# One transformer layer on one core: batches of three score groups, nine copied groups a unit, and a new order on VectorE

## The chip, the cores and the metric

The kernel runs on one core of a Trainium2 chip. A core has TensorE (matmuls; called PE in the profile, with its weight loads as PEld), ScalarE (ACT, here nearly only the exponentials), VectorE (DVE), GpSimd (POOL) and the queues that start DMAs (SyncE is SP). The engines run side by side, each through its own list of instructions in order, and wait for each other on semaphores. The metric is the device time of one launch in microseconds (us); lower is better.

## The reference

The input is x, 4096 tokens of 256 numbers, float32. `xn` is its layer norm. The output is x + attention(xn) + FFN(xn):

```
q, k, v = xn @ Wq.T, xn @ Wk.T, xn @ Wv.T          # 16 heads of 16 numbers
attention = softmax(q @ k.T / 16) @ v               # per head, 4096 x 4096 scores
scores = softmax(xn @ gate_w.T); idx = top2(scores + gate_b)
expert(x) = silu((x@w1 + b1) * (x@w3 + b3)) @ w2 + b2   # 256 -> 352 -> 256
FFN = sum over the two chosen of 8 experts of score * expert(xn)  +  shared expert(xn)
```

The work is dominated by the attention: 16 heads x 4096 x 4096 exponentials, with a small product before (q by k, 16 deep) and after each (by v, 16 wide).

## The kernel before, in words

**Attention.** A head is worked through in two sweeps, one for each half of the queries. A sweep has 32 key tiles of 128 keys (`NT`), and each key tile two score groups. A score group is 128 keys by 1024 queries: TensorE makes it with two matmuls side by side in the two halves of its rows (line 894) into two PSUM banks. There are three such pairs of banks (`SB = 3`), so group n goes where group n - 3 was. ScalarE then writes exp(group) to one of 8 slots of `probs` in SBUF (line 1198). A value step (line 907) is one key tile: it multiplies two finished groups by v, in four column strips, and adds into the one output bank (`O_BANK`). A program has 2048 score groups and 1024 value steps. The trace counts 8 matmuls per value step and 2 per score group.

**Copied groups.** For some groups (`moved(n)`) VectorE first copies the scores from PSUM to the `probs` slot (line 1773), which frees the PSUM pair; ScalarE then takes the exponential from SBUF in place (line 1194). TensorE's next use of that pair waits for the copy (`s_moved`) and not for the exponential (`s_exp`).

**FFN units.** The FFN is cut into 55 units of up to 256 tokens: 8 of the shared expert, 39 of routed tokens (the last seven, units 40 to 46, get narrower in steps of 32 columns), 8 of the shared expert. One unit is woven into 36 score groups and 18 value steps. It has three upward parts (`up_both(u, 0..2)`, line 919, 12 matmuls each) and the downward part of the unit before (`down_tile`, line 931, 18 matmuls). All go through one bank (`F_BANK`), which VectorE reads: `gate` and `product` after each upward part, `keep` after the downward part. VectorE also splits all weights and tokens into a high and a low part (`up_hi`, `up_lo`, `down_hi`, `down_lo`, `tokens_hi`, `tokens_lo`), and ScalarE adds one tanh a unit.

**Order.** It is written out by hand. On TensorE `unit(u)` is a list of `next_scores(count)`, `next_values(count)` and FFN parts. I call a run of score groups with what follows it up to the next run a batch. On VectorE a loop over u lists the FFN steps, `move_scores(u, place)` for each copied place of the unit, and `after_values(m)`, which does what is due once m value steps are finished: `take_output` (line 1620, a transpose that empties the output bank at the end of a sweep), `add_output` two value steps later, and `next_v` (v of the next head). Before the first value step of a sweep TensorE waits for `take_output` (`s_osb`). The two wait rules that matter are these:

```
# next_scores: group n needs the pair of group n - 3
if n >= SB and moved(n - SB): pe.wait_ge(s_moved, moved_up_to(n - SB))
elif n >= SB:                 pe.wait_ge(s_exp, n - SB + 1)
# next_values: value step m needs groups 2m and 2m + 1
if issued[2] < 2 * m + 2:     pe.wait_ge(s_exp, 2 * m + 2)
```

**Tail.** From unit 49 on no group is copied before (`MOVE_TO = 49`). There VectorE also joins the experts' rows into the result (`join`, five tiles a unit, each two operations), with rows that GpSimd gathers.

Below, places are counted from 0 within a unit's 36 groups, in the order in which `unit(u)` issues them. The copied places before are 11, 14, 20, 23, 31 and 34 (the code's numbers are one higher, and `moved` takes the one off).

## Time and profile before

| what | value |
|---|---|
| median of 3 runs | 2106.71 us (2106.71 to 2111.02) |
| profiled execution: time, span of the core | 2107.03 us, 2105.1 us |
| TensorE matmuls busy | 2076.8 us, 99% |
| ScalarE busy | 2008.4 us, 95% |
| VectorE busy | 1141.8 us, 54% |
| granted TensorE clock, mean | 0.999 of full |
| copy of a score group (L1773), mean | 1222 ns |
| transpose of the output bank (L1620) | 0.71 us |
| `add_output`, three operations | 0.25, 0.42 and 0.43 us, 1.15 us from start to end |
| `down_hi` and `down_lo` | 0.55 and 0.96 us |
| one tile of `join`, two operations | 0.48 us each, 1.03 us together |

Matmuls are pipelined and their ends are modelled, so 99% says that TensorE hardly ever had nothing in flight, not that it ran at its peak. The difference of two start times is the safer number: it is the pace. The same holds for ScalarE, where an exponential lasts 1.05 us but the next starts earlier. All times below are from the one profiled execution.

### The profile page before, as it was taken

The page shows a single profiled execution, that of the slowest core. Times are in us where ns is not written, and L with a number is a line of the kernel's source. Part 1 is how long each engine was busy: PE and PEld are TensorE (multiplying, and loading weights), DVE is VectorE, ACT ScalarE, POOL GpSimd, SP SyncE. Part 2 cuts the span into 40 slices and gives each one's busy share as a digit, 9 for nine tenths or more (in the row PEclk, how much of TensorE's full clock was granted, in tenths as well). Part 3 has the DMA queues.
Part 4 walks back from the last instruction along what each step waited for, and adds up shares of the span by engine and source line. Part 5 has one row for each costly group of instructions (what it writes and reads, how often), then busy time and mean ns, then how long its engine had stood idle before and what let it go on. Part 6 is the DMA issues. An engine that isn't in the chain of part 4 may idle for free.

```text
span 2105.1 us, 38572 instructions
## 1 busy us (share of the span) xinstructions
PE 2076.8 (99%) x15722; PEld 968.1 (46%) x15722; DVE 1141.8 (54%) x1843; ACT 2008.4 (95%) x2228; POOL 250.7 (12%) x260
## 2 busy tenths in 40 slices
PE   9999999999999999999999999999999999999998
PEld 6734444444444444444444444444444444444442
DVE  8554555555555555555555555555555554544531
ACT  6799999999999999999999999999999999999998
POOL 0307764000000000000000000000000000122220
PEclk9999999999999999999999999999999999999999
DMA  8874433222222212132222231313132221323331
GB/s 290 284 257 120 123 123 102 60 57 70 67 73 63 71 49 81 52 79 61 65 60 72 67 73 55 85 44 80 52 80 62 70 70 57 100 73 89 99 99 35
DMA packets 223352, 187.82 MB, mean 89 GB/s; under 512 B 110471, under 2 KB 192190, under 8 KB 223174
## 3 DMA queue, kind: packets, MB, share of 16 engines
q1 hardware_dynamic: 209350, 148.68, 25.0%
q0 software_dynamic: 12496, 36.34, 5.3%
q8 instruction: 124, 2.03, 0.4%
q14 instruction: 54, 0.44, 0.1%
q10 hardware_dynamic: 1328, 0.33, 0.1%
HBM read 130.21 MB, written 55.05 MB: 88 GB/s over the span
## 4 chain that ended last, share of the span: by engine, by line
PE 88%; ACT 6%; DVE 4%; DMA 1%; issue 1%; SPq 0%; another core or an unknown queue 0%; DVEq 0%; ACTq 0%
PE PS L907 41%; PE PS L894 28%; PE PS L919 12%; PE PS L931 6%; ACT probs L1198 5%; ACT probs L1194 1%; DMA qk_parts<-part_a 1%; DVE probs L1773 1%; DVE stats L1324 0%; DVE o_t L1620 0%; PE PS L684 0%; DVE probs L1348 0%; DVE x_parts L1360 0%; PE PS L798 0%; DVE w_hi L1688 0%
## 5 line engine op out<-in xcount | busy, mean ns | idle before, releaser
L1198 ACT ACTIVATE probs<-PS 128x1024 f32<-128x1024 f32 x1766 | 1679.6, 1053 | 58.0 <-PE PS L894 45.6
L907 PE MATMUL PS<-probs,v_head 128*32 128x512 f32 x8192 | 989.6, 599 | 10.7 <-DVE o_t L1620 7.2
L894 PE MATMUL PS<-q_ring,k_stack 50*128 50x512 f32 x4096 | 697.8, 436 | 6.4 <-ACT probs L1198 4.6
L894 PEld LDWEIGHTS PS<-q_ring,k_stack 50*128 50x128 f32 x4096 | 333.5, 184 | 542.1 <-ACT probs L1198 471.6
L1773 DVE COPY probs<-PS 128x1024 f32<-128x1024 f32 x282 | 344.6, 1222 | 186.7 <-PE PS L894 185.7
L907 PEld LDWEIGHTS PS<-probs,v_head 128*32 128x32 f32 x8192 | 210.0, 108 | 482.1 <-issue 372.8
L1194 ACT ACTIVATE probs<-probs 128x1024 f32<-128x1024 f32 x282 | 301.4, 1069 | 2.4 <-DVE probs L1773 2.1
L1661 DVE TENSOR_SCALAR gate_in<-PS,bias_sb 128x256 f32<-128x256 f32 (+7 forms) x165 | 76.3, 463 | 370.9 <-PE PS L919 364.0
L919 PE MATMUL PS<-x_hi,w_hi 128*128 128x256 f32 (+9 forms) x660 | 199.3, 302 | 0.0
L1270 POOL DMA_DIRECT2D slot_y<-y_sb x39 | 27.9, 716 | 1387.3 <-DVE y_sb L1731 1351.7
L919 PE MATMUL PS<-x_hi,w_lo 128*128 128x256 f32 (+9 forms) x660 | 184.4, 279 | 0.0
L919 PE MATMUL PS<-x_lo,w_hi 128*128 128x256 f32 (+9 forms) x660 | 184.2, 279 | 0.0
L919 PEld LDWEIGHTS PS<-x_hi,w_hi 128*128 128x128 f32 (+1 forms) x660 | 118.6, 180 | 58.1 <-issue 58.1
L1671 DVE SCALAR_TENSOR_TENSOR hid<-hid,prod 128x768 f32<-128x768 f32 (+7 forms) x55 | 49.9, 907 | 131.4 <-ACT hid L1179 131.4
L919 PEld LDWEIGHTS PS<-x_lo,w_hi 128*128 128x128 f32 (+1 forms) x660 | 118.8, 180 | 0.0
L919 PEld LDWEIGHTS PS<-x_hi,w_lo 128*128 128x128 f32 (+1 forms) x660 | 118.8, 180 | 0.0
L931 PE MATMUL PS<-w_hi,hid_hi 128*128 128x256 f32 (+4 forms) x318 | 95.4, 300 | 0.0
L1692 DVE TENSOR_TENSOR w_lo<-w_raw,w_hi 128x1408 fp32r<-128x1408 f32 x55 | 89.9, 1635 | 0.2
L931 PE MATMUL PS<-w_lo,hid_hi 128*128 128x256 f32 (+4 forms) x318 | 89.8, 282 | 0.0
L931 PE MATMUL PS<-w_hi,hid_lo 128*128 128x256 f32 (+4 forms) x318 | 89.7, 282 | 0.0
L1666 DVE SCALAR_TENSOR_TENSOR prod<-PS,bias_sb,gate_in 128x256 f32<-128x256 f32 (+7 forms) x165 | 76.8, 466 | 5.9
L1261 POOL DMA_INDIRECT slot_x<-y_sb,pos x64 | 73.9, 1155 | 19.1 <-issue 14.0
(201 smaller groups left out, 1238.8 us busy)
## 6 DMA issues: line engine op xcount, KB each, us to landing
w_raw<-in_w SPq DMA_DIRECT2D x110, 352.0 KB
k_stack<-qk_parts SPq DMA_DIRECT2D x120, 128.0 KB
w_raw<-in_w SPq DMA_DIRECT2D x55, 256.0 KB
q_ring<-qk_parts SPq DMA_DIRECT2D x372, 32.0 KB
qk_parts<-part_a SPq DMA_DIRECT2D x20, 512.0 KB, 4.9
slot_x<-early_sq SPq DMA_DIRECT2D x39, 256.0 KB, 3.6
slot_in<-slot_x SPq DMA_DIRECT2D x156, 64.0 KB, 2.5
slot_y<-y_sb POOLq DMA_DIRECT2D x39, 256.0 KB, 2.5
```

What stands on the lines that cost most here:

```text
L894: last = pe.matmul(bank(2 * score_buffer(turn, g) + r), k_stack[rows, kt * P:(kt + 1) * P], q_ring[rows, sweep, i * QC:(i + 1) * QC], star ...
L907: last = pe.matmul(bank(O_BANK)[VW * j:VW * (j + 1), :], v_head[:, kt, :], probs[:, slot, (j % 2) * QC:(j % 2 + 1) * QC], start=(kt == 0), ...
L919: last = pe.matmul(f_half(w)[0:FT[j], 0:width(u)], a[u % 2][:, w, dt, j * P:j * P + FT[j]], b[:, dt * CH:dt * CH + width(u)], start=(n == ...
L931: last = pe.matmul(f_half(t)[0:own, :], a[0:rows, j, t * P:t * P + own], b[0:rows, j, :], start=(n == 0), stop=(n == 8))
L1194: nc.scalar.activation(probs[:, prob_slot(g), :], probs[:, prob_slot(g), :], ACT.Exp, scale=ENERGY_SCALE).then_inc(s_exp, 1)
L1198: nc.scalar.activation(probs[:, prob_slot(g), :], bank(2 * score_buffer(h, g), 2), ACT.Exp, scale=ENERGY_SCALE).then_inc(s_exp, 1)
L1261: nc.gpsimd.indirect_dma_start(out=slot_x, out_offset=bass.IndirectOffsetOnAxis(ap=pos[:, u * TPU + t, k:k + 1], axis=0), in_=rows[:, t, : ...
L1661: V.tensor_scalar(gate_in[0:FT[j], 0:width(u)], f_half(0)[0:FT[j], 0:width(u)], bias_sb[0:FT[j], u % 2, j:j + 1], 0.5, ALU.add, ALU.mult). ...
L1666: V.scalar_tensor_tensor(prod[u % 2][0:FT[j], j, 0:width(u)], f_half(1)[0:FT[j], 0:width(u)], bias_sb[0:FT[j], u % 2, 3 + j:4 + j], gate_i ...
L1671: V.scalar_tensor_tensor(hid[:, :, 0:width(u)], hid[:, :, 0:width(u)], 1.0, prod[u % 2][:, :, 0:width(u)], ALU.add, ALU.mult).then_inc(s_h ...
L1692: V.tensor_tensor(w13_lo[u % 2][:, :, :, :], w13_raw[:, :, :, :], w13_hi[u % 2][:, :, :, :].bitcast(f32), ALU.subtract).then_inc(s_w13, 1)
L1773: V.tensor_copy(probs[:, prob_slot(g), :], bank(2 * score_buffer(h, g), 2)).then_inc(s_moved, 1)
```

## The change: three groups in every batch, other copied places, another order on VectorE

On TensorE a unit becomes twelve batches of three groups. Before it had thirteen (ten of three, three of two). The eighteen value steps follow in eight runs, two of three and six of two; before it was nine of two. The first unit starts one group earlier, and the one group left over stands behind the last unit.

```
-FIRST_GROUPS = 2 * FIRST_VALUES + 3
+FIRST_GROUPS = 2 * FIRST_VALUES + 2
-TANH_AT = 39
-MOVED = (12, 15, 21, 24, 32, 35)
+TANH_AT = 41
+MOVED = (2, 8, 17, 20, 23, 26, 29, 32, 35)
-MOVE_TO = 49
+MOVE_TO = 55
 def unit(u):
-    next_scores(2)
+    next_scores(3)
     up_both(u, 0)
-    next_scores(2)
-    next_values(2)
+    next_scores(3)
+    next_values(3)
     next_scores(3)
     up_both(u, 1)
-    next_scores(2)
-    next_values(2)
     next_scores(3)
-    next_values(2)
-    next_scores(3)
-    next_values(2)
+    next_values(3)
     next_scores(3)
...
-    next_scores(2)
+    next_scores(3)
     up_both(u, 2)
...
-    next_scores(1)
+    next_scores(3)
+    next_values(2)
```

The copied places are now 2, 8, 17, 20, 23, 26, 29, 32 and 35: the last group of nine of the twelve batches. Copies run from unit 2 to unit 54. On VectorE `take_output` leaves `after_values` and becomes `take_values(m)`, and the loop is listed anew:

```
+def take_values(m):
+    if (m - 1) % NT + 1 == NT:
+        take_output((m - 1) // NT)
 for u in range(UNITS + 1):
+    move_scores(u, 2)
     gate(u, 0); product(u, 0)
+    take_values(m + 2); after_values(m + 2); join(u, 1); move_scores(u, 8)
+    gate(u, 1); product(u, 1); hidden(u - 1); take_values(m + 4)
+    hidden_hi(u - 1); hidden_lo(u - 1); take_values(m + 6); after_values(m + 4)
+    up_hi(u + 1); up_lo(u + 1); keep(u - 1); move_scores(u, 17); after_values(m + 6)
+    down_hi(u); down_lo(u); take_values(m + 8); move_scores(u, 20); after_values(m + 8); join(u, 1)
+    take_values(m + 10); move_scores(u, 23); turn_tokens(u + 1); after_values(m + 10)
+    take_values(m + 12); move_scores(u, 26); gate(u, 2); product(u, 2); move_scores(u, 29)
+    after_values(m + 12); tokens_hi(u + 1); take_values(m + 14); tokens_lo(u + 1)
+    move_scores(u, 32); after_values(m + 14); join(u, 1); take_values(m + 16)
+    move_scores(u, 35); after_values(m + 16); join(u, 2); take_values(m + 18); after_values(m + 18)
```

TensorE's list from the end of a unit's first upward part to its second, before:

```order
L919 MATMUL PS<-x_hi,w_lo 128x256
L894 MATMUL PS<-q_ring,k_stack 128x512 x4
L907 MATMUL PS<-probs,v_head 32x512 x8
L894 MATMUL PS<-q_ring,k_stack 128x512 x6
L919 MATMUL PS<-x_hi,w_hi 128x256
```

The same place now:

```order
L919 MATMUL PS<-x_hi,w_lo 128x256
L894 MATMUL PS<-q_ring,k_stack 128x512 x6
L907 MATMUL PS<-probs,v_head 32x512 x12
L894 MATMUL PS<-q_ring,k_stack 128x512 x6
L919 MATMUL PS<-x_hi,w_hi 128x256
```

Two score matmuls are one group and four value matmuls one value step in this list. The run of two groups has become one of three, and the run of two value steps one of three.

VectorE's list in unit 34, from the copy behind the third upward part on; a sweep ends before the unit's seventeenth value step. Before:

```order
L1773 COPY probs<-PS 128x1024 [waits s_scores]
L1712 CAST x_hi<-x_t 128x512 [waits s_ab,s_tt]
L1716 TENSOR_TENSOR x_lo<-x_t,x_hi 128x512 [waits s_xhi]
L1773 COPY probs<-PS 128x1024 [waits s_scores]
L1620 STREAM_TRANSPOSE o_t<-PS 128x512 [waits s_pv]
L1500 COPY v_head<-v_all 128x8x16 [waits s_pv]
L1625 RECIPROCAL rec<-o_t 128x16 [waits s_osb]
```

Now:

```order
L1774 COPY probs<-PS 128x1024 [waits s_scores]
L1710 CAST x_hi<-x_t 128x512 [waits s_ab,s_tt]
L1714 TENSOR_TENSOR x_lo<-x_t,x_hi 128x512 [waits s_xhi]
L1774 COPY probs<-PS 128x1024 [waits s_scores]
L1618 STREAM_TRANSPOSE o_t<-PS 128x512 [waits s_pv]
L1774 COPY probs<-PS 128x1024 [waits s_scores]
L1498 COPY v_head<-v_all 128x8x16 [waits s_pv]
L1623 RECIPROCAL rec<-o_t 128x16 [waits s_osb]
```

The transpose now stands ahead of the copy of the last batch (place 35) and behind that of the batch before it. Before, it stood behind the copy of the last batch.

VectorE's list in unit 24, where a sweep ends before the unit's fifth value step. Before:

```order
L1666 SCALAR_TENSOR_TENSOR prod<-PS,bias_sb,gate_in 128x256 [waits s_gin]
L1620 STREAM_TRANSPOSE o_t<-PS 128x512 [waits s_pv]
L1688 CAST w_hi<-w_raw 128x1408 [waits s_w13r]
L1773 COPY probs<-PS 128x1024 [waits s_scores]
L1500 COPY v_head<-v_all 128x8x16 [waits s_pv]
L1625 RECIPROCAL rec<-o_t 128x16 [waits s_osb]
L1627 TENSOR_TENSOR early_sq<-o_t,rec 128x256 [waits s_loop_a]
L1632 TENSOR_TENSOR resid<-resid,early_sq 128x16x16 [waits s_resid,s_norm]
L1773 COPY probs<-PS 128x1024 [waits s_scores]
```

Now, from the hidden step to the first copy behind the downward weights:

```order
L1669 SCALAR_TENSOR_TENSOR hid<-hid,prod 128x768 [waits s_tanh]
L1618 STREAM_TRANSPOSE o_t<-PS 128x512 [waits s_pv]
L1674 CAST hid_hi<-hid 128x512 [waits s_hid]
...
L1774 COPY probs<-PS 128x1024 [waits s_scores]
L1498 COPY v_head<-v_all 128x8x16 [waits s_pv]
L1623 RECIPROCAL rec<-o_t 128x16 [waits s_osb]
L1625 TENSOR_TENSOR early_sq<-o_t,rec 128x256 [waits s_loop_a]
L1630 TENSOR_TENSOR resid<-resid,early_sq 128x16x16 [waits s_resid,s_norm]
L1694 CAST w_hi<-w_raw 128x768 [waits s_w2r]
L1698 TENSOR_TENSOR w_lo<-w_raw,w_hi 128x768 [waits s_w2h]
L1774 COPY probs<-PS 128x1024 [waits s_scores] x2
```

The fifth value step now lies inside a run of three (steps 4 to 6), so nothing of TensorE's stands between the end of the sweep and the step that waits for the transpose. And `add_output` now stands, with the split of the downward weights, between the copies of places 17 and 20.

## Rows read from the trace of the kernel before

**Rows 1.** Chain of work that ended last, unit 25: start us, us, engine and line, matmuls.
```profile
1003.35 1.62 PE PS L919 x12
1004.98 0.66 PE PS L894 x4
1005.64 1.85 PE PS L907 x16
1007.49 0.89 PE PS L894 x6
...
1010.00 0.78 PE PS L894 x4
...
1019.02 2.35 PE PS L931 x18
...
1030.28 1.59 PE PS L919 x12
...
1038.26 1.62 PE PS L919 x12
```

**Rows 2.** Timeline of ScalarE, unit 25: start, us, engine, line, count, [idle before <-releaser].
```profile
1007.48 0.92 ACT L1179 ACTIVATE hid<-prod 128x768 f32<-128x768 f32 x1
1008.21 6.83 ACT L1198 ACTIVATE probs<-PS 128x1024 f32<-128x1024 f32 x7
...
1021.84 1.94 ACT L1198 ACTIVATE probs<-PS 128x1024 f32<-128x1024 f32 x2 [0.34 <-PE PS L894]
```

**Rows 3.** Timeline of TensorE and VectorE, same unit, behind the downward part.
```profile
1021.30 0.96 PE L894 MATMUL PS<-q_ring,k_stack 50*128 50x512 f32 x6
...
1022.31 1.22 DVE L1773 COPY probs<-PS 128x1024 f32<-128x1024 f32 x1 [0.21 <-PE PS L894]
```

**Rows 4.** Timeline of ScalarE near the end, an unbroken run of exponentials.
```profile
2073.93 24.86 ACT L1198 ACTIVATE probs<-PS 128x1024 f32<-128x1024 f32 x27 [1.62 <-PE PS L894]
```

**Rows 5.** Timeline of unit 25, a score group that waits for an exponential.
```profile
1010.27 0.19 PEld L894 LDWEIGHTS PS<-q_ring,k_stack 50*128 50x128 f32 x2 [0.16 <-ACT probs L1198]
```

**Rows 6.** Timeline of unit 8, a value step that waits for an exponential.
```profile
417.89 0.96 PE L894 MATMUL PS<-q_ring,k_stack 50*128 50x512 f32 x6
417.92 1.06 ACT L1194 ACTIVATE probs<-probs 128x1024 f32<-128x1024 f32 x1 [0.32 <-DVE probs L1773]
...
418.89 1.92 ACT L1198 ACTIVATE probs<-PS 128x1024 f32<-128x1024 f32 x2
...
419.94 0.16 PEld L907 LDWEIGHTS PS<-probs,v_head 128*32 128x32 f32 x8 [1.01 <-ACT probs L1198]
...
420.70 1.06 ACT L1194 ACTIVATE probs<-probs 128x1024 f32<-128x1024 f32 x1
...
420.94 0.96 PE L894 MATMUL PS<-q_ring,k_stack 50*128 50x512 f32 x6
421.65 2.85 ACT L1198 ACTIVATE probs<-PS 128x1024 f32<-128x1024 f32 x3
```

**Rows 7.** Timeline of unit 34, the end of a sweep.
```profile
1350.19 1.22 DVE L1773 COPY probs<-PS 128x1024 f32<-128x1024 f32 x1 [0.46 <-PE PS L894]
1351.33 0.71 DVE L1620 STREAM_TRANSPOSE o_t<-PS 128x512 f32<-128x512 f32 x1
...
1352.09 1.92 PE L907 MATMUL PS<-probs,v_head 128*32 128x512 f32 x16 [1.94 <-DVE o_t L1620]
```

**Rows 8.** Chain of work, unit 49, where no group is copied.
```profile
1852.70 1.12 PE PS L894 x6
```

**Rows 9.** Timeline of TensorE: first upward part of units 2, 40, 49 and 54.
```profile
192.84 0.39 PE L919 MATMUL PS<-x_hi,w_hi 128*128 128x256 f32 x1
...
1530.01 0.37 PE L919 MATMUL PS<-x_hi,w_hi 128*128 128x224 f32 x1
...
1840.60 0.39 PE L919 MATMUL PS<-x_hi,w_hi 128*128 128x256 f32 x1
...
2021.96 0.39 PE L919 MATMUL PS<-x_hi,w_hi 128*128 128x256 f32 x1
```

More of the change, by code:

```diff
@@ L110, in moved @@
 def moved(n):
-    u, place = divmod(n - FIRST_GROUPS + 1, UNIT_GROUPS)
+    u, place = divmod(n - FIRST_GROUPS, UNIT_GROUPS)
     return MOVE_FROM <= u < MOVE_TO and place in MOVED
@@ L121, in moved_group @@
 def moved_group(u, place):
-    return unit_start(u) - 1 + place
+    return unit_start(u) + place
 def shared_loads(u):
@@ L1045, in _ @@
                 unit(u)
+            next_scores(1)
             for n in range(6):
@@ L1754, in after_values @@
                     add_output(n - 1)
-                if kt == NT:
-                    take_output(n)
-                elif n % 2 == 1 and n < SWEEPS - 1 and kt % KTB == 0:
+                if kt < NT and n % 2 == 1 and n < SWEEPS - 1 and kt % KTB == 0:
                     next_v(n // 2, kt // KTB - 1)
+            def take_values(m):
+                if (m - 1) % NT + 1 == NT:
+                    take_output((m - 1) // NT)
             def join(u, count):
@@ L1789, in _ @@
                     product(u, 0)
+                take_values(m + 2)
+                after_values(m + 2)
+                join(u, 1)
+                move_scores(u, 8)
+                if real:
+                    gate(u, 1)
+                    product(u, 1)
                 if u:
                     hidden(u - 1)
-                after_values(m + 2)
+                take_values(m + 4)
                 if u:
@@ L1795, in _ @@
                     hidden_lo(u - 1)
-                if real:
-                    gate(u, 1)
-                    product(u, 1)
+                take_values(m + 6)
                 after_values(m + 4)
@@ L1801, in _ @@
                     up_hi(u + 1)
-                move_scores(u, 12)
-                after_values(m + 6)
-                move_scores(u, 15)
-                if more:
                     up_lo(u + 1)
-                after_values(m + 8)
-                join(u, 2)
                 if u == 0:
@@ L1822, in _ @@
                     counts()
-                after_values(m + 12)
+                take_values(m + 8)
+                move_scores(u, 20)
+                after_values(m + 8)
                 join(u, 1)
+                take_values(m + 10)
+                move_scores(u, 23)
                 if routed(u + 1):
                     turn_tokens(u + 1)
-                after_values(m + 14)
+                after_values(m + 10)
+                take_values(m + 12)
+                move_scores(u, 26)
                 if real:
@@ L1830, in _ @@
                     product(u, 2)
-                move_scores(u, 32)
+                move_scores(u, 29)
+                after_values(m + 12)
                 if more:
                     tokens_hi(u + 1)
+                take_values(m + 14)
+                if more:
                     tokens_lo(u + 1)
@@ L1838, in _ @@
                     experts_of_tiles()
+                move_scores(u, 32)
+                after_values(m + 14)
+                join(u, 1)
+                take_values(m + 16)
                 move_scores(u, 35)
                 after_values(m + 16)
-                join(u, JOINS - 3)
+                join(u, 2)
+                take_values(m + 18)
                 after_values(m + 18)
```

8 lines of the change are left out of this document (4 added, 4 removed).

## The prediction

> **What bounds the kernel now.** I read the page first (TensorE 99% busy, ScalarE 95%, VectorE 54%), then the chain of waits over one ordinary unit, then the timelines of ScalarE and VectorE beside it, and last the starts of all units. In the chain of unit 25 every piece is TensorE's [rows 1]. The reader should see the pace: a batch of three groups takes 0.89, of two 0.66, a run of two value steps 1.85, an upward part 1.62 (the third 1.59), the downward part 2.35. Ten of three, three of two, nine value runs, the FFN parts: 8.9 + 2.0 + 16.7 + 4.8 + 2.35 = 34.75, and one group that waits 0.12 (0.78 instead of 0.66). The unit lasts 1038.26 - 1003.35 = 34.91. So an ordinary unit is bound by TensorE. ScalarE is close behind. Exponentials from PSUM come every (24.86 - 1.04) / 26 = 0.916 [rows 4], a tanh takes 1008.21 - 7.48 = 0.73 [rows 2]. A copied group costs more: from 417.92 to 418.89 is 0.97, though the next scores were there at 418.43, and from 420.70 to 421.65 it is 0.95 with the next there at 421.48 [rows 6]; I take 0.95. That makes 30 x 0.916 + 6 x 0.95 + 0.73 = 33.9 of the 34.9. The missing 1.0 are idle gaps behind the three FFN parts, of which the row behind the downward part shows one [rows 2].
>
> This is a loop of two engines that each have under 3% to spare. The copies and the waits decide which one yields.
>
> **Four delays that I need.** Let T be the start of a batch. (a) The first group reaches ScalarE at T + 0.54 (1021.30 to 1021.84), the third reaches VectorE at T + 1.01, its copy lasts 1.22 and ScalarE starts some 0.13 later, so T + 2.36 [rows 2, 3]. (b) A score group starts 1.15 after the start of the exponential that frees its banks: the sixth group's began at 1008.21 + 0.91 = 1009.12, the load follows at 1010.27 [rows 2, 5]. Groups two and three of a batch start at T + 0.23 and T + 0.46 when nothing holds them. (c) A value step starts 1.05 after its exponential (418.89 to 419.94) and then needs 1.00 to the end of the run [rows 6]. The batch of that row began at 417.89 and should have handed over at 417.89 + 0.89 + 1.85 = 420.63; it did at 420.94. So the second value step of a pair holds TensorE once its exponential starts later than T + 0.69. (d) From the end of a sweep's last value step to the first of the next, the transpose between them included, is 0.9: 0.76 from the transpose's start (1351.33 to 1352.09) [rows 7], and some 0.13 before it as in (a).
>
> **Part 1: fewer switches on TensorE.** A group costs 0.89 - 0.66 = 0.23, so a batch carries 0.20 besides its groups. A value step costs 1.85 - 1.00 = 0.86, so a run carries 0.13. One batch and one run less: -0.33. A run of three is not in the trace; it lies between 1.85 + 0.86 = 2.71 and two runs' price of 1.85 + 1.00 = 2.85. I take 2.71, the nearer rows. The unit becomes 12 x 0.89 + 6 x 1.85 + 2 x 2.71 + 4.8 + 2.35 = 34.4 if nothing waits, 0.45 less than 34.91 with the 0.12 of today gone too. With the upper price it is 34.7.
>
> **Part 2: what ScalarE takes back.** Three exponentials with a copied one need 2 x 0.916 + 0.95 = 2.78, uncopied 2.75. Follow a unit, with b how late ScalarE is against T + 0.54. Behind the downward part (batch length 0.89 + 2.35 = 3.24) it is on time. Three batches with a pair of value steps last 2.75 each, and b grows to 0.05 to 0.09. The batch with the third upward part lasts only 0.89 + 1.59 = 2.48 and now brings three groups instead of two: b = 0.35. After two more batches b is 0.40, and there the last pair needs the exponential of place 33, started at T + 0.54 + 0.40 = T + 0.94. By (c) TensorE waits 0.25. The next two upward parts (2.51 a batch) push b up again, while a run of three (3.6) lets ScalarE catch up. On the way (b) caps b near 0.40: a second group waits 0.03 to 0.04 in the batch of place 4 and about 0.12 in that of place 10. The run of three itself does not wait: its third step is due at T + 0.89 + 1.72, its exponential starts by T + 0.94. Sum of waits 0.40 of the 0.45 gained. An ordinary unit becomes 34.83 (34.45 + 0.38), 0.07 less than before. From the other side: 27 x 0.916 + 9 x 0.95 + 0.73 = 34.0 of work and 0.5 idle in each of the two long batches at places 9 and 12 is 34.9 to 35.0. I keep 34.83, with 34.45 and 34.98 as ends. Over units 2 to 39: -0.07 x 38 = -2.7, ends -17 and +3.
>
> On the copies the Trainium skill has a rule against this change (VectorE: DVE Perf Modes, section on the TRN2 errata): ScalarE pays 224 cycles besides the elements when it reads SBUF and 172 when it reads PSUM, at 1.2 GHz. The trace agrees: 0.95 to 0.97 against 0.916. By that rule three more copied groups cost 3 x 0.043 = 0.13 a unit, by the rows 3 x 0.034 to 0.054, and my sum would be 1 us longer over these units.
>
> **Part 3: VectorE's order.** Copies add 3 x 1.22 = 3.7 to some 20 a unit, which VectorE has. What counts is whether each starts at T + 1.01. In an ordinary unit I find it does: the dense stretch (second gate, hidden parts, upward weights, `keep`) now holds no copy, and the split of the downward weights ends 1.5 behind the copy of place 17, about 0.1 before that of place 20 is due. So this costs nothing, with 0.1 to spare there.
>
> At the end of a sweep it does count. Before, the first upward parts of units 2 and 40 are 1337.17 apart [rows 9]; 38 x 34.90 = 1326.2, so 11.0 is lost. Three times 2.0 of it are units 2, 18 and 34, where the transpose stood behind a copy: in unit 34 the copy starts at 1350.19, the transpose at 1351.33, and TensorE stood idle for 1.94 [rows 7]. Those 6.1 go: the transpose is now ahead. So do 0.7 to 1.6 in each of units 4 and 20 and 36. Against that:
> - Units 17 and 33: the sweep ends inside a run of three, with no batch between. By (d) 0.9 plus the 0.13 of a new run, 1.0 each.
> - Units 8, 24 and 40: the same, and `add_output` (1.15) plus the downward weights (1.5) now stand between the copies of places 17 and 20. The copy is 1.1 late and ScalarE with it, so the pair with place 21 waits about 0.8 more: 2.0 each.
> - Units 6, 22 and 38: the transpose waits behind `down_lo` and comes at T + 0.9 instead of T + 0.13: 0.85 each.
> - Units 11, 13, 27, 29: 0.1 to 0.3 each.
>
> Units 2 to 39: 2.0 + 4.0 + 2.55 + 0.8 = 9.4 against 11.0, that is -1.6. Ends: -6, if late copies find slack, and +5, if each of these turns costs a whole 2.0.
>
> **Part 4: the rest.** Units 40 to 48 took 310.6 [rows 9]. The narrow ones are near ScalarE's limit (about 34.1 a unit), so little changes, and unit 40 gets a late sweep: +1.0. Units 49 to 53 took 181.4, 36.3 each [rows 9]. Without copies three or four batches a unit wait 0.23 (1.12 instead of 0.89) [rows 8]; these waits go. With `join` squeezed in the copy of place 2 is 0.5 late, about +0.35 a unit. At 34.83 + 0.35 and 1.0 for the sweep in unit 49, five units take 177, -4.3. But some 2.6 of the 181.4 are two hold-ups of TensorE's batches in units 49 and 51 that no copy explains, and I can't say that they go; I take -3.0, ends 0 and -5. Start, units 0 and 1, and tail: +0.5.
>
> **Sum.** -2.7 - 1.6 + 1.0 - 3.0 + 0.5 = -5.8 against this execution's 2107.03 (span 2105.1), which is 0.3 above the median: 2101.2 us.
>
> **The rivals.** First, TensorE stays the bound and ScalarE keeps up. For it: ScalarE has 1.0 idle a unit today, and the loss of 0.25 hangs on a threshold read at one place. Against it: three groups behind the third upward part are one more than before. It gives 34.45 a unit: -17 instead of -2.7, 2087. Second, on the other side: the sweep ends. VectorE's late copies and a transpose with nothing to cover it cost 2.0 in each of the eight units 6, 8, 17, 22, 24, 33, 38 and 40, 16 against the 11.0 lost before, the ordinary unit stays at 34.9 and the late units give nothing: with 0.8 for the small turns and 0.5 at the ends about +6, 2113. For it: before, a transpose behind one copy cost 2.0 [rows 7]. Against it: the same order frees the units that lost most. It decides, at 34.9 a unit, once these eight cost over 1.2 each on average. Third, nothing measurable: ScalarE takes back all of part 1 (34.9) and the late units gain as little as the sweeps lose, 2106.
>
> **How the numbers follow.** A measurement of this kernel can tell about 0.2%, 4.2 us: faster is below 2102.5. My forecast has 0.5, with a spread of 4 about it: 0.3 faster, 0.19 the same, 0.01 slower. The first rival has 0.2 (faster), the second 0.17 (0.03 the same, 0.14 slower), the third 0.13 (0.11 the same, 0.02 slower). Together 0.5 faster, 0.33 the same, 0.17 slower. The range of 2089 to 2111 leaves out the better half of the first rival and the worse half of the second.
>
> **What would show it.** Right, if the chain of an ordinary unit shows the last pair of value steps (place 33) longer than 1.85 and ScalarE idle only behind the two runs of three and the downward part; if the unit lasts 34.8; if the 2.9 batches of units 2, 18 and 34 are gone; and if units 8 and 24 show a late copy of place 20. Wrong, if ScalarE still idles behind the third upward part (then 34.5), if a run of three takes over 2.8, or if a copy in an ordinary unit starts after T + 1.1.

## The result, and the profile after

The changed kernel takes 2117.88 us (median of 5 runs, 2116.30 to 2120.46). The kernel before, run beside it, takes 2109.18 (2106.71 to 2113.64). The ratio is 1.0041, 95% interval 1.0025 to 1.0058: slower by 0.4%, where 2101.2 and a gain were forecast. The profiled execution took 2117.15 (span 2115.2) against 2107.03 of before, +10.1.

The busy times of the page do not show where that is: TensorE and ScalarE are as busy as before. The chain of work that ended last does look different. From the page of the changed kernel, parts 1 and 4, and part 4 of the kernel before:

```profile
PE 2070.7 (98%) x15722; PEld 974.3 (46%) x15722; DVE 1378.8 (65%) x2038; ACT 2006.8 (95%) x2228; POOL 244.9 (12%) x260
...
PE 50%; ACT 42%; DVE 5%; issue 1%; another core or an unknown queue 1%; DMA 1%; SPq 0%; DVEq 0%; ACTq 0%
...
PE 88%; ACT 6%; DVE 4%; DMA 1%; issue 1%; SPq 0%; another core or an unknown queue 0%; DVEq 0%; ACTq 0%
```

ScalarE's share has gone from 6% to 42%, and 1% is time whose end nothing in the trace explains ("another core or an unknown queue"). The starts of the units show where the time went. These rows of TensorE's timeline, changed kernel, are the first upward parts of units 2, 40, 49 and 54 and answer [rows 9]:

```profile
194.37 0.38 PE L919 MATMUL PS<-x_hi,w_hi 128*128 128x256 f32 x1
...
1525.73 0.37 PE L919 MATMUL PS<-x_hi,w_hi 128*128 128x224 f32 x1
...
1838.34 0.39 PE L919 MATMUL PS<-x_hi,w_hi 128*128 128x256 f32 x1
...
2028.73 0.39 PE L919 MATMUL PS<-x_hi,w_hi 128*128 128x256 f32 x1
```

From such differences, in every profiled execution (us; the last column runs to the end of the span):

| kernel | set | units 0, 1 | 2 to 39 | 40 to 48 | 49 to 53 | unit 54 and tail |
|---|---|---|---|---|---|---|
| before | 0 | 70.9 | 1337.2 | 310.6 | 181.4 | 83.1 |
| changed | 1 | 73.4 | 1331.4 | 312.6 | **190.4** | **86.5** |
| spread_joins | 2 | 73.4 | 1330.7 | 312.5 | 176.5 | 83.1 |
| late_nocopy | 2 | 73.4 | 1331.3 | 313.9 | 183.1 | 83.4 |
| before_burst | 2 | 70.9 | 1338.0 | 310.6 | 190.9 | 83.0 |
| direct_rows | 2 | 73.4 | 1331.3 | 312.6 | 176.9 | 82.7 |
| paced_gathers | 3 | 73.4 | 1331.0 | 312.5 | 176.9 | 82.8 |
| sweep_order | 3 | 73.4 | 1327.7 | 313.2 | 190.6 | 85.9 |
| short_tanh | 3 | 73.4 | 1328.9 | 313.7 | 194.2 | 86.0 |
| spread_turns_from_1 | 3 | 72.0 | 1328.2 | 311.8 | 183.4 | 83.4 |
| burst_alone | 4 | 73.4 | 1331.3 | 312.6 | 176.9 | 82.8 |
| burst_no_copies | 4 | 73.4 | 1330.7 | 314.2 | 183.0 | 83.4 |
| paced_order_from_1 | 4 | 71.8 | 1328.2 | 311.8 | 177.3 | 82.1 |
| thin_joins | 5 | 73.4 | 1330.7 | 312.5 | 175.1 | 82.7 |
| few_rows | 5 | 73.4 | 1330.7 | 312.5 | 176.9 | 82.7 |

"Set" says which kernels were run together, from set 1 on with the kernel before beside them; set 0 are the three runs of the kernel before ahead of the prediction (median 2106.71 us), from which its trace is. Beside the others the kernel before took 2109.18 us in set 1, 2104.40 in set 2, 2109.31 in set 3, 2103.97 in set 4 and 2102.73 in set 5. The changed kernel itself was run in set 1 alone. This matters for the late units, as shown below.

So the body gained 5.8 and the late units lost 9.0, the tail 3.3, the first two units 2.5, units 40 to 48 2.0. The start gained 1.0.

**The ordinary unit** lasts what was forecast. The chain of the changed kernel in unit 25, beside [rows 1] (start us, us, engine and line, count):

```profile
1004.18 2.71 PE PS L907 x24
...
1009.40 0.97 PE PS L894 x6
1010.37 2.71 PE PS L907 x24
...
1013.98 2.35 PE PS L931 x18
1016.33 0.45 PE PS L894 x2
...
1016.80 1.94 ACT probs L1196 x2
1018.74 0.95 ACT probs L1192
1019.68 1.82 ACT probs L1196 x2
...
1033.56 0.92 ACT probs L1196
1034.48 0.04 issue
1034.52 1.06 PE PS L907 x8
```

A run of three value steps takes 2.71. The batch of place 9 takes 0.97 instead of 0.89. The last pair starts at 1033.38 and the next scores at 1035.52, 2.14 instead of 1.85; the chain shows its second step waiting for the exponential. And from the first group behind the downward part (1016.80) to that exponential's end (1034.48) the chain is ScalarE's alone: 17.7 of the unit's 34.8 us. TensorE sets the pace in the other half, with the runs of three and the first, second and downward FFN parts. So the unit now has two halves with different limits, where before all of it was TensorE's [rows 1]. In ScalarE's half three exponentials with a copied one take 2.77 (1.82 and 0.95), while TensorE needs 2.75 for a batch with a pair of value steps and 2.48 for the one with the third upward part. ScalarE falls behind by that, until the last pair waits 0.29 for it. A saving on TensorE in that half would buy nothing. ScalarE's timeline there has only two gaps, one behind a run of three and one behind the downward part, beside [rows 2]:

```profile
1010.28 2.99 ACT L1196 ACTIVATE probs<-PS 128x1024 f32<-128x1024 f32 x3
1013.55 2.86 ACT L1196 ACTIVATE probs<-PS 128x1024 f32<-128x1024 f32 x3 [0.27 <-PE PS L894]
1016.80 1.94 ACT L1196 ACTIVATE probs<-PS 128x1024 f32<-128x1024 f32 x2 [0.39 <-PE PS L894]
```

Unit 34, which stood 1.94 [rows 7], now takes the transpose ahead of the copy; TensorE's next value steps follow 0.77 later, and the unit lasts 34.81:

```profile
1347.09 0.72 DVE L1618 STREAM_TRANSPOSE o_t<-PS 128x512 f32<-128x512 f32 x1 [0.65 <-PE PS L907]
1347.86 2.21 PE L907 MATMUL PS<-probs,v_head 128*32 128x512 f32 x16
1347.95 1.22 DVE L1774 COPY probs<-PS 128x1024 f32<-128x1024 f32 x1
```

**The late units.** Units 49 to 53 take 35.89, 38.49, 36.65, 39.30 and 40.06 (before 36.72, 35.87, 37.10, 35.96, 35.71). I call it a hold-up when TensorE's results reach the other engines late and TensorE then runs dry. Timeline behind the start of unit 52 (1949.37), changed kernel:

```profile
1952.60 0.48 DVE L1743 SCALAR_TENSOR_TENSOR resid<-y_sb,weight,resid 128x256 f32<-128x256 f32 x1
...
1954.60 0.96 PE L894 MATMUL PS<-q_ring,k_stack 50*128 50x512 f32 x6
1954.67 0.87 ACT L1177 ACTIVATE hid<-prod 128x768 f32<-128x768 f32 x1
...
1958.27 1.94 ACT L1196 ACTIVATE probs<-PS 128x1024 f32<-128x1024 f32 x2 [2.73 <-remote]
1958.42 1.23 DVE L1774 COPY probs<-PS 128x1024 f32<-128x1024 f32 x1 [5.34 <-remote]
1959.35 0.50 PE L894 MATMUL PS<-q_ring,k_stack 50*128 50x512 f32 x2 [2.17 <-ACT probs L1196]
...
1961.20 4.12 PE L907 MATMUL PS<-probs,v_head 128*32 128x512 f32 x24
```

The three score groups were issued at 1954.60. By the four delays of the prediction ScalarE should have had the first at 1955.14 (it was done with its tanh at 1955.54) and VectorE the third at 1955.61. Both got theirs at 1958.3 and 1958.4, together; "remote" means that the trace has no releaser for that moment. The trace does keep the moments at which TensorE's signals for finished score groups came: 1958.25, 1958.29 and 1958.33, and the signal for the upward part issued behind them at 1958.46. In unit 25 such signals are 0.23 apart, and an upward part takes TensorE 1.62. Three groups 0.04 apart and an upward part 0.13 behind them can't be the pace of the work. It was done by then, and the signals came late and all at once. TensorE then ran dry. The granted clock also fell, after TensorE had been idle from 1957.2 to 1959.3. The columns are window, its length, busy time (count) of PE, PEld, DVE, ACT and POOL, clock, DMA share, GB/s.

```profile
1954.00:1958.00 4.00, 3.17 (x26) 1.97 (x18) 0.00 (x0) 1.54 (x2) 2.21 (x3) 1.00 0.59 174
1958.00:1962.00 4.00, 2.24 (x10) 0.68 (x14) 3.51 (x6) 3.73 (x5) 0.00 (x0) 0.82 0.12 45
1962.00:1966.00 4.00, 4.00 (x30) 1.21 (x22) 3.76 (x6) 2.10 (x4) 0.00 (x0) 0.76 0.00 0
```

1.00 is the 2.4 GHz level; 0.82 and 0.76 are stretches partly at 1.2 GHz, and the run of three at 1961.20 took 4.05 to the next scores, not 2.71. Such hold-ups end at 1883.2 (named "PE PS L894" by the trace), 1921.3, 1958.3, 1993.3 to 1995.3 and 2037. Beside each of them GpSimd was issuing indirect gathers for `join` without a break, in the same stretch:

```profile
1946.25 0.95 POOL L1298 DMA_INDIRECT y_sb<-slot_y,pos  x1 [8.66 <-DVE resid L1743]
...
1949.53 1.01 POOL L1298 DMA_INDIRECT y_sb<-slot_y,pos  x1 [0.30 <-PE PS L894]
1950.85 0.95 POOL L1298 DMA_INDIRECT y_sb<-slot_y,pos  x1 [0.30 <-issue]
...
1955.87 0.95 POOL L1298 DMA_INDIRECT y_sb<-slot_y,pos  x1 [0.30 <-issue]
```

That is a run of six 1.25 apart, with two more and a plain load just ahead. From unit 49 on the kernel before had eleven runs of four and none longer. The change made the longer runs: of five tiles a unit it joins one behind copy 32, two behind copy 35 and one behind the next unit's value steps (1945.0 to 1953.1 in this stretch), and each join frees a buffer for two gathers.

**Where the late signals appear.** Late signals are in the traces of sets 0, 1 and 3 alone. The rows below are read from the recorded moments of TensorE's score signals. "Latest" is the longest time, from unit 48 on, between the start of a group's last matmul and its signal; the signal behind the last scores of the kernel is left out. In units 10 to 39 it is 0.52 at most in every trace. The last column counts the recorded signals of units 1 to 4, 144 groups whose place lies long before any join.

| set | time of before | kernel | longest run of gathers | smallest distance of two signals | latest | recorded in units 1 to 4 |
|---|---|---|---|---|---|---|
| 0 | 2106.71 | before | 4 | 0.04 | 1.97 | 132 |
| 1 | 2109.18 | changed | 8 | 0.04 | 4.31 | 127 |
| 3 | 2109.31 | sweep_order, short_tanh | 8 | 0.04 | 4.55, 4.44 | 123, 126 |
| 3 | | spread_turns_from_1 | 4 | 0.04 | 1.58 | 125 |
| 3 | | paced_gathers | 2 | 0.04 | 0.57 | 129 |
| 2, 4, 5 | 2102.73 to 2104.40 | all nine | up to 10 | 0.22 | 0.65 | 144 each |

In sets 2, 4 and 5 no signal was late, in no kernel and with runs of up to ten gathers, and the kernel before took 2.3 to 6.6 us less. What differs between the sets is not known; sets 3 and 4 ran on the same chip. So kernels of sets 0, 1 and 3 can be compared, and there the signals are the later the longer the run of gathers is. But a hold-up that is missing in a kernel of sets 2, 4 or 5 may be missing because of the set: the changed kernel was not run beside it.

### The profile page after: what moved, and what is told of

The parts are those of the page before. It is cut to its first block, busy times and chain, and to the rows that moved or that the text cites. A ratio compares the mean times of both kernels' runs of the same rounds, so it can differ in the third digit from the quotient of the medians.

```text
span 2115.2 us, 38791 instructions
## 1 busy us (share of the span) xinstructions
PE 2070.7 (98%) x15722; PEld 974.3 (46%) x15722; DVE 1378.8 (65%) x2038; ACT 2006.8 (95%) x2228; POOL 244.9 (12%) x260
## 4 chain that ended last, share of the span: by engine, by line
PE 50%; ACT 42%; DVE 5%; issue 1%; another core or an unknown queue 1%; DMA 1%; SPq 0%; DVEq 0%; ACTq 0%
ACT probs L1196 29%; PE PS L907 21%; PE PS L894 15%; ACT probs L1192 12%; PE PS L919 8%; PE PS L931 6%; DVE probs L1774 1%; DVE stats L1322 0%; DVE o_t L1618 0%; DMA qk_parts<-part_a 0%; DVE probs L1346 0%; DVE w_lo L1698 0%; DVE x_parts L1358 0%; PE PS L798 0%
## 5 line engine op out<-in xcount | busy, mean ns | idle before, releaser
L1196 ACT ACTIVATE probs<-PS 128x1024 f32<-128x1024 f32 x1571 | 1543.4, 1086 | 66.1 <-PE PS L894 57.0
L1774 DVE COPY probs<-PS 128x1024 f32<-128x1024 f32 x477 | 583.1, 1222 | 459.0 <-PE PS L894 439.2
L894 PE MATMUL PS<-q_ring,k_stack 50*128 50x512 f32 x4096 | 679.9, 432 | 12.2 <-ACT probs L1196 8.5
L894 PEld LDWEIGHTS PS<-q_ring,k_stack 50*128 50x128 f32 x4096 | 339.2, 184 | 483.5 <-ACT probs L1196 402.9
L1192 ACT ACTIVATE probs<-probs 128x1024 f32<-128x1024 f32 x477 | 534.3, 1120 | 6.6 <-DVE probs L1774 5.5
L931 PEld LDWEIGHTS PS<-w_hi,hid_hi 128*128 128x128 f32 (+4 forms) x318 | 59.4, 187 | 20.0 <-issue 19.9
L1259 POOL DMA_INDIRECT slot_x<-y_sb,pos x64 | 65.8, 1028 | 19.1 <-issue 14.6
```

What stands on the lines that cost most here:

```text
L894: last = pe.matmul(bank(2 * score_buffer(turn, g) + r), k_stack[rows, kt * P:(kt + 1) * P], q_ring[rows, sweep, i * QC:(i + 1) * QC], star ...
L931: last = pe.matmul(f_half(t)[0:own, :], a[0:rows, j, t * P:t * P + own], b[0:rows, j, :], start=(n == 0), stop=(n == 8))
L1192: nc.scalar.activation(probs[:, prob_slot(g), :], probs[:, prob_slot(g), :], ACT.Exp, scale=ENERGY_SCALE).then_inc(s_exp, 1)
L1196: nc.scalar.activation(probs[:, prob_slot(g), :], bank(2 * score_buffer(h, g), 2), ACT.Exp, scale=ENERGY_SCALE).then_inc(s_exp, 1)
L1259: nc.gpsimd.indirect_dma_start(out=slot_x, out_offset=bass.IndirectOffsetOnAxis(ap=pos[:, u * TPU + t, k:k + 1], axis=0), in_=rows[:, t, : ...
L1774: V.tensor_copy(probs[:, prob_slot(g), :], bank(2 * score_buffer(h, g), 2)).then_inc(s_moved, 1)
```

## The experiments

**spread_joins.** One join moved to each of two quieter places.

```
     hidden_lo(u - 1)
+    join(u, 1)
     take_values(m + 6)
...
     move_scores(u, 23)
+    join(u, 1)
...
     after_values(m + 16)
-    join(u, 2)
```

> The changed kernel with the five joined tiles of a unit set further apart: one each behind the value-step work of step 2, behind hidden_lo, behind the copies of places 20, 23 and 32, and none behind the copy of place 35. Theory burst: in the changed kernel three tiles are joined within 7 us around the end of a unit, GpSimd then issues six to eight gathers back to back, and while they are in flight signals between the engines come up to 3 us late, which the copies of units 49 to 54 can't absorb. Then the runs of six gathers go, the waits for a remote signal go, units 49 to 53 fall from 190.4 to 175-180 us, and the kernel gains 9 to 14 us against the changed one. Theory copies: VectorE is simply overloaded by nine copies and five tiles a unit; then moving tiles about gives under 3 us.

Measured 2100.36 us (2100.00 to 2101.83, before beside it 2104.4; ratio 0.9982, 0.9973 to 0.9992). Units 49 to 53 took 36.94, 34.84, 34.76, 34.81, 35.10, with no idle time "<-remote"; the runs of gathers are of four at most. This is set 2, so it does not show that spreading the joins removes the hold-ups. With the joins spread in set 3 (spread_turns_from_1 below) units 49 to 53 took 183.4.

**late_nocopy.** `MOVE_TO = 49`: copies end where they ended before, joins stay bunched.

> The changed kernel with no copied groups from unit 49 on, as in the kernel before; joins stay where the change has them. Theory burst: the hold-ups stay, units 49 to 53 take 185 to 195 us. Theory copies: the overload is gone, units 49 to 53 take 178 to 183 us as before the change (181.4).

2107.43 us (ratio 1.0014, 1.0005 to 1.0024). Units 49 to 53: 183.1, with two unbroken runs of six, two more broken by a plain load, and no idle "<-remote". My expectation for bunching alone (185 to 195) missed. That the copies are needed for a hold-up does not follow: this is set 2, and the kernel before had late signals in units 49 and 51 with no copies at all. A unit without copies takes 36.37 against 34.82, so the copies are worth 1.55 a unit where nothing holds TensorE up.

**before_burst.** The kernel before with its five joins at the unit's end (`join(u, JOINS)` in the last place, the others out).

> The kernel before, but all five joined tiles of a unit in one place, at the unit's end, so that GpSimd gets work for several tiles at once. Theory burst: runs of six gathers appear, and units 49 to 53 grow from 181.4 by 3 to 15 us. Theory copies: no copied group is near, so they stay within 2 us of 181.4.

2118.35 us (ratio 1.0066, 1.0049 to 1.0083), units 49 to 53 190.9. But no signal was late there (0.65 at most), with runs of up to ten gathers. The loss is another one: VectorE stood in its joins for rows that had not landed ("<-DMA", up to 5.28), and the chain runs through it:

```profile
1995.93 0.48 DVE L1743 SCALAR_TENSOR_TENSOR resid<-y_sb,weight,resid 128x256 f32<-128x256 f32 x1 [5.28 <-DMA y_sb<-slot_y,pos]
```

So here the 9.5 us more than in the kernel before go with the wait for the rows that follows from joining five tiles at once with three buffers. The run has nothing to say on late signals.

**direct_rows.** Same bytes, same places, by plain loads of neighbouring rows.

```
-    nc.gpsimd.indirect_dma_start(
-        out=got[b][:, k, :], out_offset=None, in_=slot_y,
-        in_offset=bass.IndirectOffsetOnAxis(ap=pos[:, c, k:k + 1], axis=0)).then_inc(s_got[b], 16)
+    nc.gpsimd.dma_start(got[b][:, k, :], slot_y[(c + k) * P:(c + k + 1) * P, :]).then_inc(s_got[b], 16)
```

> The changed kernel with each indirect gather of 128 rows replaced by one plain transfer of 128 neighbouring rows of the same tensor from the same queue; the rows joined are not the ones that the routing picks. Count, places and bytes stay. Theory burst, because of gathering: the late signals go although the joins stay bunched, units 49 to 53 take 174 to 179 us. If bunched transfers of any kind cause it, they stay at 185 to 192 us. Theory copies: no change, 190.

2100.43 us (ratio 0.9982, 0.9972 to 0.9991), units 49 to 53 176.9, no hold-up, with the joins as bunched as in the changed kernel. This is set 2 as well, so whether the indirect kind of the transfers is part of the cause is not shown.

**paced_gathers.** The joins stay bunched; each gather waits for a place of its own (`gather_at` replaces the wait for `GATHER_FROM + GATHER_STEP * ...`).

```
+def gather_at(c, k):
+    if c < GB:
+        return GATHER_FROM + GATHER_STEP * (TOP * c + k)
+    q, i = divmod(c, JOINS)
+    place = ((-2, -2), (5, 8), (11, 14), (17, 20), (24, 28))[i][k]
+    return unit_start(SZ + 2 + q) + place
```

> The changed kernel with its joins where they are (three tiles within some 7 us), but each tile's two indirect gathers held back to places of their own in the unit, at most two back to back; bytes, copies, joins and VectorE's order stay. Theory A (TensorE's signals come late when GpSimd issues indirect gathers in an unbroken run): units 49 to 53 fall from 190.4 to about 177 us, with no idle time '<-remote' of over 1 us on ScalarE and VectorE, and the time is 2104 (against 2117 unpaced). Theory B (the joins themselves, six operations on VectorE in a row with the copies of places 32, 35 and 2 around them, and the gathers are only incidental): units 49 to 53 stay at 188 to 192 and the time at 2116. direct_rows spoke for A, but it took away the indirect kind of transfer as well; this one keeps it.

2100.19 us (2100.12 to 2100.44; before beside it 2109.31; ratio 0.9958, 0.9941 to 0.9975). Units 49 to 53 took 176.9, and in the profiled executions 17.0 us are gone against the changed kernel (2117.15 to 2100.12), 13.5 of them in units 49 to 53 and 3.7 behind them. This is the experiment that counts, for the kernels beside it in set 3 that keep the runs of eight did have the hold-ups: sweep_order with 190.6 us in units 49 to 53 and a time never below 2112.32 in ten executions, short_tanh with 194.2. The copies, the joins and their places are those of the changed kernel. So in such a set the crowding of the gathers costs some 13.5 us, and neither the bunched joins by themselves nor an overload of VectorE by the copies does.

**sweep_order.** At the ends of sweeps.

```
-    after_values(m + 6)
     down_hi(u)
-    down_lo(u)
-    take_values(m + 8); move_scores(u, 20); after_values(m + 8)
+    take_values(m + 8); move_scores(u, 20); down_lo(u)
...
     move_scores(u, 23)
+    after_values(m + 6); after_values(m + 8)
```

> The changed kernel with another order on VectorE at the ends of sweeps: the transpose due behind the eighth value step now stands ahead of the split of the downward weights' low part, and add_output and next_v of places 4 and 8 behind the copy of place 23, so that nothing but the low part stands between the copies of places 17 and 20. Theory (the turns of units 8, 24 and 40 cost 1.8 because the copy of place 20 is late, those of 6, 22 and 38 cost 0.7 because the transpose waits behind down_lo): units 8, 24, 40 fall from 36.7 to about 35.8 and units 6, 22, 38 from 35.5 to 34.9; units 2 to 39 take 1327.5 to 1328.5 instead of 1331.4. Rival (a sweep end inside a run of three costs what it does by the transpose alone): no more than 0.3 of it goes, 1331. Units 49 to 53 keep their 190, so the time is 2113 to 2116.

2115.41 us (2112.32 to 2120.44; ratio 1.0029, 1.0018 to 1.0039). Units 8, 24 and 40 fell from 36.67, 36.79 and 36.65 to 35.86, 35.88 and 35.87, units 6, 22 and 38 from 35.5 to 34.8, units 2 to 39 by 3.7 (3.3 against paced_gathers beside it). In the changed kernel the copy of place 20 (T = 983.26, due at 984.27) and what it holds:

```profile
985.33 1.22 DVE L1774 COPY probs<-PS 128x1024 f32<-128x1024 f32 x1
...
986.58 1.06 ACT L1192 ACTIVATE probs<-probs 128x1024 f32<-128x1024 f32 x1 [0.82 <-DVE probs L1774]
...
988.61 1.06 PE L907 MATMUL PS<-probs,v_head 128*32 128x512 f32 x8 [0.51 <-ACT probs L1196]
```

and in sweep_order, where T = 982.76:

```profile
983.76 1.22 DVE L1774 COPY probs<-PS 128x1024 f32<-128x1024 f32 x1 [1.05 <-PE PS L894]
...
985.13 1.08 ACT L1192 ACTIVATE probs<-probs 128x1024 f32<-128x1024 f32 x1
```

**short_tanh.** The slice of `hid` in the tanh is `0:BL` instead of `0:width(u)` from unit 1 on.

> The changed kernel with ScalarE's tanh cut to 32 of the unit's 256 columns from the second unit on (the other columns keep what was there, so the FFN's output is not the reference's). ScalarE has some 0.5 to 0.6 us less to do in each unit, right behind the sixth group. My account of the ordinary unit (TensorE sets the pace, and ScalarE's lateness costs 0.04 at place 4, 0.12 at place 10, 0.25 to 0.3 at place 33, the last of them well ahead of the tanh) expects only the wait at place 10 to go: the unit falls from 34.82 to 34.70 or so. If ScalarE as a whole set the pace it would fall by 0.5, to 34.3; if it were TensorE alone, by nothing.

One run, 2119.76 us (the hold-ups differ). The 25 ordinary units among 5 to 38 took 34.73 on average instead of 34.82. The batch of place 9 lost its wait (0.97 to 0.90), the last pair kept 2.13. So of the 0.5 less work on ScalarE the unit gained 0.09, the wait at place 10, which I had put at 0.12. It does not show that TensorE paces the whole unit: the tanh stands in the half where TensorE does, and ScalarE's half behind the downward part kept its length.

**spread_turns_from_1.** spread_joins, sweep_order, `MOVE_FROM = 1`, and the experts of the tiles behind the last copy of unit 1.

> spread_joins with the order of sweep_order, copies from unit 1 on instead of unit 2, and the experts of the tiles worked out behind the last copy of unit 1. Against spread_joins (0.9982 of before): units 2 to 39 lose 3 us as in sweep_order, units 0 and 1 together 1 to 2 us (73.4 to 72), so 2096 to 2097, ratio 0.996. If the sweep ends cost what they do by the transpose alone, 2099 and ratio 0.9975.

2102.04 us (2101.09 to 2103.28; ratio 0.9965, 0.9952 to 0.9977). Units 2 to 39 lost 2.5 and units 0 and 1 1.4 against spread_joins, as expected, but units 50 to 53 took 36.1 to 37.5: hold-ups again, smaller, with runs of no more than four gathers:

```profile
1972.52 0.48 DVE L1659 TENSOR_SCALAR gate_in<-PS,bias_sb 96x256 f32<-96x256 f32 x1 [1.96 <-remote]
1972.56 1.94 ACT L1196 ACTIVATE probs<-PS 128x1024 f32<-128x1024 f32 x2 [0.91 <-PE PS L894]
```

Here, in set 3, runs of four are enough for signals 1.6 late.

**burst_alone.** paced_gathers, but for the first three tiles `return unit_start(SZ + 1) + 1` and the load of unit 50 issued ahead: six gathers in a row in a unit without joins.

> paced_gathers, with only the first six gathers changed: they no longer come three score groups apart in units 47 and 48 but in one unbroken run at the start of unit 48. That unit has copies, but no join: VectorE does nothing with the rows there. Theory A (an unbroken run of six indirect gathers is enough to make TensorE's signals late): unit 48 takes 37 to 39 us instead of 34.79, with ScalarE or VectorE idle '<-remote' for over 1 us within 3 to 9 us of the run's start. Rival (it needs the joins on VectorE beside it, so that engine's own order or port is part of the cause): unit 48 stays at 34.8 to 35.0. All other units as in paced_gathers (units 49 to 53 at 177).

2100.23 us. Unit 48 took 34.81, and nothing waited:

```profile
1803.61 1.02 POOL L1309 DMA_INDIRECT y_sb<-slot_y,pos  x1 [4.98 <-PE PS L903]
1804.93 0.99 POOL L1309 DMA_INDIRECT y_sb<-slot_y,pos  x1 [0.30 <-issue]
...
1809.99 0.95 POOL L1309 DMA_INDIRECT x_t<-slot_y,pos  x1 [0.31 <-PE PS L903]
```

In set 4 this decides nothing on Theory A: there no kernel had a late signal.

**burst_no_copies.** The same with `MOVE_TO = 48`.

> burst_alone with no copied groups from unit 48 on (the burst of six gathers in unit 48 stays). A unit without copies takes 36.4 (late_nocopy, which had runs of six in two such units and no hold-up). If the copies are needed for the hold-up: unit 48 at 36.3 to 36.6 without idle time '<-remote'. If the run of gathers is enough: 38 or more, with such idle time.

2108.09 us; unit 48 took 36.54, no hold-up. It adds nothing on late signals, since this is set 4 too and burst_alone had none either.

**thin_joins.** `row = resid[:, c, 0:HD]` and `got[b][:, k, 0:HD]` in the join, all else as in the changed kernel.

> The changed kernel with each join's two VectorE operations on 16 of the 256 columns (the other columns get nothing, so the output is not the reference's). Joins, gathers, copies and all their places stay. burst_alone showed that a run of six gathers without joins beside it holds nothing up. If VectorE's part (its operations of 0.48 us reading what the gathers have just written) is what is missing there, the hold-ups go and units 49 to 53 take 177 to 180. If it is the gathers' and the other transfers' meeting in that stretch, they stay: 187 to 192, with idle time '<-remote' of 2 to 5 us.

2097.58 us, units 49 to 53 35.89, 34.82, 34.79, 34.80, 34.80. The gathers are where they were, in the same run:

```profile
1939.74 0.94 POOL L1298 DMA_INDIRECT y_sb<-slot_y,pos  x1 [8.67 <-DVE resid L1743]
...
1943.01 0.97 POOL L1298 DMA_INDIRECT y_sb<-slot_y,pos  x1 [0.30 <-PE PS L894]
1944.29 0.95 POOL L1298 DMA_INDIRECT y_sb<-slot_y,pos  x1 [0.30 <-issue]
...
1949.30 0.95 POOL L1298 DMA_INDIRECT y_sb<-slot_y,pos  x1 [0.30 <-PE PS L894]
```

and the copy that VectorE reached 5.34 late in the changed kernel follows its scores:

```profile
1949.66 1.23 DVE L1774 COPY probs<-PS 128x1024 f32<-128x1024 f32 x1 [3.09 <-PE PS L894]
```

As this is set 5, the missing hold-ups say nothing on the width of the joins. What it does show, against few_rows beside it, is what VectorE's time in the joins costs: 176.9 against 175.1, all of it in units 51 and 53 (35.8 and 35.6 against 34.8).

**few_rows.** `[0:32]` rows in each gather and its offsets.

> The changed kernel with each indirect gather cut to 32 of its 128 rows (the other rows are not fetched, so the output is not the reference's). GpSimd issues the same number of gathers in the same places, with a quarter of the row transfers. If what counts is that GpSimd has a gather in hand without a break, the hold-ups stay: units 49 to 53 at 187 to 192. If it is the row transfers (their number or their bytes in the queue), they go: 176.5 to 178.

2099.72 us, units 49 to 53 176.9, no hold-up, with GpSimd's runs as long as in the changed kernel (1.16 apart instead of 1.25). Set 5 again: the part that the rows play is not shown.

**paced_order_from_1.** paced_gathers, sweep_order, `MOVE_FROM = 1` (the experts of the tiles behind the last copy of unit 1).

> paced_gathers with the order of sweep_order at the ends of sweeps and copies from unit 1 on. Paced_gathers took 2100.19 (0.9958 of before). The order took 3.3 us off units 2 to 39, copies in unit 1 another 1.4; the gathers stay apart, so units 49 to 53 should stay at 177. Expected 2095.5 us, ratio 0.9935. If units 49 to 53 come out at 183 again as in spread_turns_from_1, the order of VectorE in the late units (joins ahead of add_output) and not the run of gathers is what holds TensorE up, and the time is 2101.

2094.85 us (2094.20 to 2095.68, 5 runs; before beside it 2103.97; ratio 0.9957, 0.9944 to 0.9971). It beats both kernels. Its ratio looks no better than that of paced_gathers because the kernel before took 5.3 us more in set 3. In its own set burst_alone, which differs from paced_gathers in six gathers, took 2100.23: 5.4 us go to the order at the ends of sweeps and to the copies of unit 1. Units 49 to 53 at 177.3 leave the rival of its expectation open, since nothing in set 4 was held up.

## Why the prediction was wrong

| term of the sum | forecast | measured |
|---|---|---|
| ordinary unit | 34.83 (-0.07 a unit) | 34.82 (-0.09) |
| units 17, 33 over that | 1.0 each | 1.02, 1.06 |
| units 8, 24, 40 | 2.0 each | 1.85, 1.97, 1.57 (unit 40 against itself before) |
| units 6, 22, 38 | 0.85 each | 0.68, 0.67, 0.74 |
| units 2 to 39 in all | -4.3 | -5.8 |
| units 40 to 48 | +1.0 | +2.0 |
| units 49 to 53 | -3.0, ends 0 and -5 | **+9.0** |
| start, units 0 and 1, tail | +0.5 | +4.9 (-1.0, +2.5, +3.3) |

**Parts 1 to 3 held.** The run of three at 2.71, the last pair over 1.85 (2.14, a wait of 0.29 for the 0.25 forecast), two of ScalarE's three gaps (the first run of three left none), the freed units 2, 18 and 34 (34.86, 34.81, 34.82 from 36.9) and the late copy of place 20 are all in the trace, and sweep_order took the causes of units 8, 24 and 40 and of 6, 22 and 38 away one for one. Part 3 priced the late copy of unit 40 at 2.0 and the sum took 1.0 for it; that is part of why units 40 to 48 came out 1.0 over. None of the three rivals happened. The first (34.45 a unit) was 0.37 off. The second forecast the right side for a wrong reason: the eight turns cost 1.2 on average, but the ordinary unit gained.

**The step that failed is Part 4**, which says of units 49 to 53 that "five units take 177" and then "I take -3.0, ends 0 and -5". The 177 was the right price of the units themselves: 176.9 with the gathers paced. Even the 0.35 a unit for `join` was right in sum (1.8 in all, by thin_joins). What I priced of `join` was VectorE's time (0.35 a unit). What I left out is what a join issues through the engine behind it: two indirect gathers on GpSimd for each freed buffer. Four tiles joined within some 8 us mean six to eight gathers in a row. The five units took 190.4, 9.0 more than before, and in set 3 the same joins with the gathers held apart took 13.5 less than that. My text noted two hold-ups in units 49 and 51 "that no copy explains". They were the sign, each 6 behind the start of a run of four gathers. In the kernel before:

```profile
1854.67 1.08 POOL L1300 DMA_INDIRECT y_sb<-slot_y,pos  x1 [16.11 <-DVE resid L1745]
...
1860.53 0.69 DVE L1725 TENSOR_TENSOR resid<-resid,PS 128x512 f32<-128x512 f32 x1 [5.09 <-remote]
...
1911.33 1.10 POOL L1300 DMA_INDIRECT x_t<-slot_y,pos  x1 [1.26 <-DVE resid L1745]
...
1917.10 1.94 ACT L1198 ACTIVATE probs<-PS 128x1024 f32<-128x1024 f32 x2 [1.40 <-remote]
```

The signals there came 0.04 to 0.05 apart as well (1860.45 to 1860.57, and 1917.03 to 1917.12). I left them as given and set an end of 0 to the loss, when an unexplained wait that the change's own moves could multiply called for an open end on the slow side. The tail's +3.3 is the same thing (the run of eight gathers at 2025 and the hold-up that ends at 2037): 3.7 of it went with paced_gathers. Without the hold-ups the time is what was forecast, 2100.2 us in paced_gathers against 2101.2. That is in part luck: the late units gained 4.5 and not 3.0, units 2 to 39 gained 6.2 and not 4.3, and units 0 and 1 lost 2.5 that the sum did not have.

**Units 0 and 1** are a second, smaller miss. They have no copies, and I had put their batches of three at nothing. Unit 1 went from 35.59 to 37.51. With copies in it, and the experts of the tiles moved to its end, it takes 35.96 (paced_order_from_1), but unit 2 then takes 35.78 instead of 34.93, so 0.7 of the 1.6 is a net gain. The two edits were made together, so what each is worth is not shown.

**Why TensorE's signals come late stays open.** Shown is this much. In sets 0, 1 and 3, and in no other, signals come late and then together while GpSimd issues indirect gathers. The delay grows with the length of the runs: 0.57 with two in a row, 1.6 to 2.0 with four, 4.3 to 4.6 with six to eight. By their spacing it is the signals that are late and not TensorE's work. Copies of score groups beside the gathers are not needed, since the kernel before had none there. Not every run of gathers does it: of the eleven runs of four in the kernel before only two left such a wait. The part of the DMA load, of the indirect kind, of the number of rows, of the width of the joins and of the copies in the changed kernel's larger hold-ups is not shown, because direct_rows, few_rows, thin_joins and late_nocopy ran in sets where no signal was late. Nor is it known what makes such a set, or how fast the changed kernel is in the other kind. Run together with the changed kernel in a set where that one is held up, these four would tell.

## What to carry to other kernels

When a step moves, follow what its completion frees and which engine acts on that, down to the last queue: the expensive part of a join here was the two gathers that it let loose. Give each of GpSimd's indirect transfers a place of its own: with it the kernel took 2100.2 both where the kernel before took 2109.3 (paced_gathers) and where it took 2104.0 (burst_alone). When an experiment takes a loss away, run the kernel that has the loss beside it again, or the loss may have gone by itself. An idle time "<-remote" in the kernel before is a cost with an unknown cause: before a change that crowds the same stretch, leave the range open on its side.

## What the hardware showed that I had not expected

- Beside six to eight indirect gathers in a nearly unbroken run, TensorE's signals reached ScalarE and VectorE 2.7 to 2.8 us late (1955.54 and 1955.61 against 1958.3 and 1958.4), three of them 0.04 apart; with the same transfers held apart, in a set of the same kind, the latest came 0.57 behind its matmul's start. In three of six sets of runs no signal came late at all.
- TensorE's clock fell to a mean of 0.76 and 0.82 of full over 4 us each behind such a stall, and a run of three value steps took 4.05 instead of 2.71: the stall cost more than itself. The clock was at its lower level, 1.2 GHz, from 1960.55 to 1963.96, after TensorE had been idle from 1957.2 to 1959.3 and, behind one group, for 0.41 more.
- ScalarE's recorded durations grow with its lateness while its pace does not. In unit 25 a copied group is shown with 1.06 to 1.19 us, but the next exponential always starts 0.94 to 0.95 later.
